# Another order for the preparation of an attention layer kernel

## The reference, cut to what matters

```python
q = (h @ Wq_c @ Wq_up).reshape(b, t, H, D).transpose(0, 2, 1, 3)      # b=2, t=1024, H=16, D=128
q = rmsnorm(apply_partial_rope(q, cos, sin), q_norm_w)
k_sw = rmsnorm(apply_partial_rope(h @ Wk, cos, sin), k_norm_w)
v_sw = h @ Wv
ck = rmsnorm(h.reshape(b, nb, M * HID) @ W_comp, k_norm_w)            # one key per block of 16 tokens
c_out = attend(q @ ck.T * scale, blocks that ended before the token, sink, ck)
sw_out = attend(50 * tanh(q @ k_sw.T * scale / 50), window of 64 tokens, sink, v_sw)
ao = (c_out + sw_out)                                                 # 4 groups of 4 heads
attn = einsum('btgf,gfi->btgi', ao, Wg).reshape(b, t, 1024) @ Wo
x = layernorm(x + attn)
x = layernorm(x + ternary_ffn(x))                                     # weight rounded to -1, 0, 1 times mean |weight|
```

## Time and profile before

| | us |
|---|---|
| median of 3 runs | 413.11 |
| lowest and highest | 410.56, 413.87 |
| the profiled execution's own time | 410.42 |
| its span, first to last instruction | 408.6 |
| PE busy | 362.8 (89%) |
| DVE busy | 329.2 (81%) |
| ACT busy | 294.3 (72%) |
| POOL busy | 283.6 (69%) |

### The profile page before, as it was taken

The page is one execution under the profiler, slowest core; times in us unless marked ns, Lnnn a source line. Parts: engine busy times, 40 slices in busy tenths (PEclk is TensorE's granted clock), DMA queues, the critical chain, the costliest instruction groups (busy, mean ns, idle before and its releaser), DMA issues. The chain is left out here.

```text
span 408.6 us, 8817 instructions
## 1 busy us (share of the span) xinstructions
PE 362.8 (89%) x3111; PEld 293.2 (72%) x3111; DVE 329.2 (81%) x683; ACT 294.3 (72%) x833; POOL 283.6 (69%) x188
## 2 busy tenths in 40 slices
PE   5995799958989899999999999979899999989882
PEld 4994676646858686877778787858686868677870
DVE  2685789677989898989989897989898989892523
ACT  3656774685877969696969695969788696958410
POOL 1844453074797979789897986887979797985802
PEclk9999799988999999999999999999999999999996
DMA  7994001887685766757675859595768777777340
GB/s 252 311 268 130 1 0 37 196 292 136 99 133 100 121 116 113 136 92 141 94 141 80 142 79 152 78 152 89 140 103 129 119 112 127 108 121 105 61 82 26
DMA packets 150284, 50.21 MB, mean 123 GB/s; under 512 B 138592, under 2 KB 148832, under 8 KB 149984
## 3 DMA queue, kind: packets, MB, share of 16 engines
q1 hardware_dynamic: 149424, 49.32, 64.4%
q10 hardware_dynamic: 816, 0.33, 0.3%
HBM read 11.87 MB, written 4.19 MB: 39 GB/s over the span
## 5 line engine op out<-in xcount | busy, mean ns | idle before, releaser
L1270 POOL TENSOR_TENSOR room_wg<-room_comp,keep 128x1024 f32<-128x1024 f32 x32 | 75.3, 2353 | 31.9 <-ACT room_comp L846 31.9
L1260 POOL TENSOR_TENSOR ao<-room_wg,ao 128x1024 f16<-128x1024 f32 x31 | 66.2, 2134 | 13.7 <-ACT ao L720 13.6
L680 PE MATMUL PS<-V,room_wg 128*128 128x129 f32 x512 | 66.2, 284 | 7.2 <-POOL room_wg L1270 4.4
L858 ACT ACTIVATE room_h<-PS,room_K 128x8 f32<-128x8 f32 (+7 forms) x256 | 70.8, 391 | 0.2 <-DVE room_K L1082 0.2
L680 PEld LDWEIGHTS PS<-V,room_wg 128*128 128x128 f32 x512 | 61.8, 198 | 11.3 <-POOL room_wg L1270 8.3
L858 ACT ACTIVATION_READ_ACCUMULATOR room_h<-PS,room_K 128x1 f32 x256 | 65.6, 278 | 0.0
L642 PE MATMUL PS<-Weff,aoT 128*128 128x256 f16 x512 | 60.8, 272 | 2.0 <-DMA aoT<-ao 2.0
L1276 POOL TENSOR_TENSOR ny<-nx,nu 128x16 f32<-128x16 f32 x16 | 46.6, 2916 | 19.8 <-DVE nx L1062 19.0
L642 PEld LDWEIGHTS PS<-Weff,aoT 128*128 128x128 f16 x512 | 49.7, 98 | 10.0 <-DMA aoT<-ao 3.1
L599 PE MATMUL PS<-room_h,kT 128*128 128x512 f16 x192 | 47.1, 380 | 10.4 <-DMA room_h<-room_K 9.9
L1060 DVE TENSOR_REDUCE ssq<-room_wg 128x8 f32<-128x1024 f32 x30 | 36.5, 1220 | 15.5 <-ACT room_wg L789 15.2
(11 more groups left out here) (185 smaller groups left out, 729.9 us busy)
## 6 DMA issues: line engine op xcount, KB each, us to landing
H<-in_L_attn_h SPq DMA_DIRECT2D x4, 512.0 KB, 6.3
room_wg<-in_L_attn_Wg SPq DMA_DIRECT2D x1, 2048.0 KB, 14.4
cw_rows<-staged SPq DMA_DIRECT2D x1, 2048.0 KB, 6.4
CW<-cw_rows SPq DMA_DIRECT2D x1, 2048.0 KB, 7.9
aoT<-ao SPq DMA_TRANSPOSE x128, 2.7
out<-room_wo SPq DMA_DIRECT2D x16, 128.0 KB, 2.1
CW<-in_L_attn_Wq_up SPq DMA_DIRECT2D x2, 512.0 KB, 13.7
room_wo<-in_L_attn_Wo SPq DMA_DIRECT2D x1, 1024.0 KB, 15.2
```

The costliest lines, as they stand in the source:

```text
L680: last = nc.tensor.matmul(pv, Pm[:, c, 2 * pr:2 * pr + 2, :], V[:, 2 * i + c, :], start=True, stop=True)
L858: last = nc.scalar.activation(Ec[:, 0:n, hd], bank(4 + hd // 8)[:, (hd % 8) * n:(hd % 8 + 1) * n], ACT.Exp, bias=mn[:, hd:hd + 1], accum_o ...
L1260: G.tensor_tensor(ao16[:, 1, c, :, :], ao[:, c, :, :], ao16[:, 0, c, :, :], ALU.subtract).then_inc(g_al, 1)
L1270: G.tensor_tensor(Pm[:, c, :, :], E[:, c, :, :], keep[:, :, :], ALU.mult).then_inc(g_mask, 1)
```

## The change

The same values are computed with the same number of matmuls. What moves:

- SP loads the up projection before the rope table and Wg instead of after them. It also waits for `s_keep` and `s_fw` before it reads `CW` back.
- ACT takes the squares of keys in two halves and the squares of values between H and KV copies; one sum of squares of Wg and both of Wo go between the WG copies. It squares the compressed key straight from PSUM, takes `square(0, ...)` ahead of the KT copies and `square(1, ...)` at the end of WE.
- DVE does the key norm's last multiplication before `latent_low(0)`. The sums and the rope of tile 0 stand ahead of the unit instead of behind it, the sums of tile 1 in step -1, and the scaling of values and of the sink factor at the end of step -1.
- POOL makes the table `below` and the splits of the sinks, and takes the first root before the window mask and the ternary weight (`local_tables`).
- PE makes `queries(1)` between WE and CW instead of at the start of step 0.

```diff
             sp.dma_start(wcomp_s[:, :, :], wcomp.rearrange("(m p) d -> p m d", p=P)).then_inc(s_comp, 16)
+            for r in range(2):
+                sp.dma_start(wqup_s[r * QC:(r + 1) * QC, :], wqup).then_inc(s_wq, 16)
             sp.dma_start(rope_s[:, :, :], rope_t).then_inc(s_tab, 16)
             sp.dma_start(wg_s[:, :, :], wg.rearrange("g (f p) i -> p (g f) i", p=P)).then_inc(s_wg, 16)
-            for r in range(2):
-                sp.dma_start(wqup_s[r * QC:(r + 1) * QC, :], wqup).then_inc(s_wq, 16)
...
                     sp.wait_ge(s_cww, 16)
+                    sp.wait_ge(s_keep, 1)
+                    sp.wait_ge(s_fw, 1)
...
                     t = i + 1
-                    if t:
+                    if t > 1:
                         queries(t)
...
                 if i == -1:
                     output_weights()
+                    queries(1)
...
+            def key_squares(n):
+
+                for g in range(4 * n, 4 * n + 4):
+                    copied(act, G_KV[g])
+                wait(act, s_tot, n)
+                nc.scalar.activation(sqk[:, TPB * n:TPB * (n + 1), :], K[:, TPB * n:TPB * (n + 1), :], ACT.Square).then_inc(s_sq, 1)
...
+                if (name, g) == ("H", 7):
+                    key_squares(0)
+                if (name, g) == ("KV", 4):
+                    value_squares(0)
+
+            key_squares(1)
+            act.wait_ge(s_wq, 32)
+            nc.scalar.activation(wqup_p[:, 0, :], wqup_s[:, :], ACT.Copy).then_inc(s_up, 1)
+            value_squares(1)
...
+            nc.scalar.activation(ck_sq, gbank(G_CK)[:, 0:D], ACT.Square, accum_out=ssk[:, NT:]).then_inc(s_cka, 1)
+            act.wait_ge(s_wg, 16)
+            for g in range(3):
+                squares(2 + g, wg_s[:, 4 * g:4 * g + 4, :])
+                latent(g)
+            latent(3)
+            square(0, 0)
+            square(0, 1)
+            for g in range(4):
+                act.wait_ge(s_ps, G_KT + g + 1)
+                nc.scalar.mul(*key_parts(g)[:2], wqk[:, 0:1]).then_inc(s_hi, 1)
+            act.wait_ge(s_setd, 1)
+            nc.scalar.mul(*key_parts(4)[:2], wqk[:, 0:1]).then_inc(s_hi, 1)
+            act.wait_ge(s_ss, 2)
+            for g in range(8):
+                if g == 1:
+                    squares(5, wg_s[:, 12:16, :])
+                if g in (3, 5):
+                    act.wait_ge(s_wo, 16)
+                    squares(6 + g // 4, wo_s[:, 4 * (g // 4):4 * (g // 4) + 4, :])
+                evac(G_WG + g, wgT[:, :, 2 * g * P:2 * g * P + 256], two(G_WG + g))
...
                 if i == -1:
                     output_weights()
+                    square(1, 0)
+                    square(1, 1)
...
-            latent_low(0)
-            copied(dve, G_CK)
-            link(V_.tensor_tensor(ck_sq, K[:, NT, :], K[:, NT, :], ALU.mult))
-            link(V_.tensor_reduce(ssk[:, NT:], ck_sq, AX.X, ALU.add))
-            V_.tensor_scalar(ckw[:, :], ssk[:, NT:], 1.0 / D, 1e-6, ALU.mult, ALU.add).then_inc(s_cks, 1)
             V_.tensor_tensor(K[:, 0:NT, :], K[:, 0:NT, :], ny[:, 0:NT].unsqueeze(2).to_broadcast([P, NT, D]),
                              ALU.mult).then_inc(s_kn, 1)
+            dve.wait_ge(s_cka, 1)
+            V_.tensor_scalar(ckw[:, :], ssk[:, NT:], 1.0 / D, 1e-6, ALU.mult, ALU.add).then_inc(s_cks, 1)
+            latent_low(0)
             dve.wait_ge(s_ckn, 1)
+            copied(dve, G_CK)
...
+            query_sums(0)
+            for hf in range(2):
+                rope_products(0, hf)
+            rope_sums(0)
...
+                        weights_rest(4, 5, 6, 7)
+                        query_sums(1)
...
                     value_weights(dve, lambda dst, src: V_.tensor_scalar(dst, src, v_unit, None, ALU.mult), 1)
+                    factors()
...
+            pool.wait_ge(s_ps, G_XC + 4)
+            G.tensor_copy(below, tables[:, P:].unsqueeze(1).to_broadcast([P, HEADS, NBLK])).then_inc(s_below, 1)
...
                 if i == -1:
-                    pool.wait_ge(s_setd, 2)
+                    pool.wait_ge(s_setn, 1)
                 if front:
                     pool.wait_ge(d_nq, t + 1)
                     G.tensor_tensor(ny[:, 0:HEADS], nx[:, 0:HEADS], nu[:, 0:HEADS], ALU.pow).then_inc(g_rs, 1)
+                if i == -1:
+                    local_tables()
```

More of the change, by code:

```diff
@@ L735, in _ @@
                     keys_values(act, nc.scalar.copy, s_kva, g)
[L737 to L745, removed]
+                if (name, g) == ("H", 5):
+                    act.wait_ge(s_sm, 2)
+                    nc.scalar.activation(e0[:, :], skm[:, :], ACT.Exp, scale=-1.0).then_inc(s_e, 1)
+                    nc.scalar.activation(e1w[:, :], skp[:, :], ACT.Exp).then_inc(s_e, 1)
+                    act.wait_ge(s_blk, 16)
+                    nc.scalar.activation(level[:, :], tables[:, 0:P], ACT.Copy).then_inc(s_sets, 1)
+                if (name, g) == ("H", 7):
[6 more added lines that the diff above has]
+            value_squares(1)
             def latent(g):
@@ L819, in results @@
                                          scale=ny[:, HEADS + 1:HEADS + 2]).then_inc(a_out, 1)
-                if front and i < 1:
-                    square(i + 1, 0)
-                if front:
+                if front and i > 0:
                     square(i + 1, 1)
@@ L1056, in step @@
                 t = i + 1
-                if front:
-                    for hf in range(2):
-                        dve.wait_ge(a_sq, 2 * t + hf + 1)
-                        V_.tensor_reduce(ssq[:, 8 * hf:8 * hf + 8], (sq if t else sq_first)[:, 8 * hf:8 * hf + 8, :], AX.X, ALU.add).then_inc(d_red, 1)
-                    dve.wait_ge(d_red, 2 * t + 2)
-                    V_.tensor_scalar(nx[:, 0:HEADS], ssq[:, :], SPREAD / D, SPREAD * 1e-6, ALU.mult, ALU.add).then_inc(d_nq, 1)
+                if front and i > 0:
+                    query_sums(t)
                 if ffn:
@@ L1086, in step @@
                     row_max(0)
-                if front:
-                    rope_products(0)
-                if first:
-                    weights_rest(0)
-                if mid:
+                    if front:
+                        rope_products(t, 0)
                     row_max(1)
-                if front:
-                    rope_products(1)
+                    if front:
+                        rope_products(t, 1)
                 if ffn:
@@ L1161, in step @@
                     query_rest(0)
-                    if first:
-                        weights_rest(5)
                     query_rest(1)
                     if first:
-                        weights_rest(6, 7)
+                        weights_rest(4, 5, 6, 7)
+                        query_sums(1)
                 def norms_of(sets):
@@ L1224, in _ @@
             G.memset(half[:, :], -0.5).then_inc(s_setp, 1)
+            pool.wait_ge(s_small, 48)
+            left = sinkb
+            for n in range(2):
+                G.tensor_copy(skh[:, n, :], left[:, :]).then_inc(s_sink, 1)
+                pool.wait_ge(s_sink, 2 * n + 1)
+                G.tensor_tensor(skr[:, n, :], left[:, :], skh[:, n, :], ALU.subtract).then_inc(s_sink, 1)
+                pool.wait_ge(s_sink, 2 * n + 2)
+                left = skr[:, n, :]
             for g in range(6, 8):
```

191 lines of the change are left out of this document (94 added, 97 removed).

## The result

| | before | after |
|---|---|---|
| median, on one chip in turn | 412.19 us (15 runs) | 415.47 us (15 runs) |
| ratio, 95% interval | | 1.0070 (1.0043 to 1.0098) |
| the same in two further comparisons | 411.60, 411.73 | 414.53, 414.19 |
| ratios there | | 1.0068 (1.0037 to 1.0098), 1.0064 (1.0028 to 1.0100) |
| the profiled execution's own time; span | 410.42; 408.6 | 414.93; 413.1 |

Three comparisons agree on some 3 us (2.5 to 3.3 by the medians, 2.8 by the mean of the ratios). A ratio leaves out the executions that are over 1.5% slower than the fastest of their kernel, so it can differ a little from the quotient of the medians. The prediction had 410.9 us, with 414.4 as the upper end of its range.

What follows compares the result with a forecast made beforehand. PE's idle waits before the second attention step were taken as the bound. First scores 0.6 us earlier plus step 0 1.6 us shorter gave -2.2 us, set on the 413.11 median: 410.9 us, range 407.4 to 414.4.

Steps and rivals of the forecast that it cites:

- first queries: Start of tile 0's query matmuls on PE: 39.9 instead of 40.61, 0.7 us earlier, behind the key norm and `latent_low(0)`.
- from there to WE: First queries to WE, carried by ACT's copies and squares: 15.9 us instead of 14.6, 1.2 us longer, WE at 55.8.
- WE to first scores: WE to the first scores: 22.6 us instead of 23.8, 1.2 us shorter; first scores at 78.4 against 79.07.
- step 0: First attention step: 1.6 us shorter (bounds 1.1 and 1.95), as mask, values and `divide` start sooner without tile 1's sums and power.
- the block: Before the first queries: POOL's 4.53 us subtraction of the up projection's low part holds up DVE's reciprocal root of the keys.
- The rope rival: Before the first queries: rope table lands at 29.1, not 25.6, shifting the key chain 3.5 us; +1.3, 414.4 us; chance 0.10.
- Both stalls: PE waits of 0.95 us in WE and 0.96 us in CW, both expected to go: 1.91 us.
- the last copy: Behind CW: the copy of its last group, formerly hidden by the queries, is uncovered and costs some 0.7 us.
- Steps 1 to 15: Attention steps behind step 0: they keep their lists and merely shift, with no growth.
- the change gives nothing: Rival: ACT's three sums of squares and a low clock in both places eat DVE's and POOL's gain; 413.1 us, chance 0.12.

## Why the prediction was wrong

Mean of three traces each (before: 79.07, 82.57, 82.72 for the first scores, and so on):

| | before | predicted | after |
|---|---|---|---|
| first queries | 41.07 | 39.9 | 41.17 |
| from there to WE | 15.5 | 15.9 | 15.9 |
| WE to first scores | 24.9 | 22.6 | 23.7 |
| step 0 | 19.53 | 17.9 | 19.68 |
| first scores of step 1 to the end | 310.5 | as before | 312.5 |

**First queries.** The mechanism was right: the block came, on the root, with 4.5 us, and moved into the path (0.17 us without the overlap; 2.4 us of the chain and 4.7 us of the total came back when the work went elsewhere). The chain from the rope products to the queries was 14.55 us in every trace of the changed kernel, against 14.3. What was mis-sized is its start, the rope table's landing: 25.6 in the prediction, 26.2 to 26.7 in the three traces (issued at 15.52 in the first, 10.7 us to landing), and the products started at 26.35 to 26.84. In sum +1.3 us. The rope rival had the right mechanism, but its bound (29.1) was too far; the latest start in any trace was 27.51. I had set the rule of the Trainium skill on `tensor_scalar` ("SBUF — State Buffer", section "Who interferes with whom") aside, as 0.4 us that no row showed. It was just such a step that took the whole 4.53 us; since any of them would have waited for the same end, the sum didn't change.

**To WE.** 15.9 predicted, 15.7 to 16.1 measured. Moving the three squares took 3.2 us off this way, just their 3.15. What the sum didn't ask for is what else they do: they open pauses of 0.5 to 0.9 us on PE right ahead of its longest dense stretch.

**WE to first scores.** Both stalls went and the last copy came (0.93 for my 0.7). (Two of the three traces of before have a third stall, 1.5 us in the middle of WE, which no trace of the changed kernel has; hence 24.9 and not 23.8 in the table.) But all three traces of the changed kernel had half clock inside WE, worth 1.6 to 1.7 us, which the sum did not hold. The clean length is 22.1 (the kernel with the old loads), better than my 22.6. I had costed the clock at the two places where the trace of before showed it low, and nowhere else. That the pauses set it off is not shown: of the eleven traces with all three squares between the copies seven had it and four had not, and it came in the kernel before, ahead of WE (53 to 57 us), in two of three traces. With two or three of the squares out of the way it did not come in three traces, which can be chance.

**Step 0.** The failed step. Prediction: the mask starts 1.5 us sooner, so values, `divide` and the next step follow, -1.6 us. After, the first mask did start 1.4 us sooner and the second values 1.1 us sooner, counted from the first scores. But the next step waits for something else: for the four transposes of the second tile's queries. The first is issued 11.0 us after the first scores before and after alike (90.11 and 91.38), and the last lands 19.5 and 19.7 us after them. I had read "the next step begins when the transposed queries have landed" off the trace, and then followed the other branch.

On the branch that counts the move did give something, and took it away again. The last two transposes also wait for the low parts of the queries, which DVE had ready 1.3 us sooner after the first scores with the sums gone (from 13.6 us on before, from 12.2 after). But with `queries(1)` in front of CW, CW ends right ahead of the first scores, and so the read-back of the value table is issued 6.7 us after them instead of 5.5 and lands 14.6 us after them instead of 13.4. For before and after, the read-back and the low parts:

```profile
84.56 0.38 SPq L394 DMA_DIRECT2D CW<-cw_rows  x1
92.63 2.36 DVE L1156 TENSOR_TENSOR room_K<-PS,room_K 128x1024 f16<-128x1024 f32 x2
```

```profile
87.06 0.38 SPq L397 DMA_DIRECT2D CW<-cw_rows  x1
92.59 2.36 DVE L1192 TENSOR_TENSOR room_K<-PS,room_K 128x1024 f16<-128x1024 f32 x2
```

And the four transposes (shortest, median and longest time of one issue in ns; first and last start) before, after, and with the read-back behind them:

```profile
L370 SPq DMA_TRANSPOSE room_h<-room_K x4: 1232/1280/1340, 90.1 to 95.2; - x4
L371 SPq DMA_TRANSPOSE room_h<-room_K x4: 1232/1325/2554, 91.4 to 96.6; - x4
L371 SPq DMA_TRANSPOSE room_h<-room_K x4: 1237/1328/1334, 90.7 to 94.7; - x4
```

The slow one is the second. It starts 12.3 us after the first scores in all three, and its 2.55 us end just behind the landing of the read-back. (That it was not slow before, where the read-back ran beside it for another 1.1 us, I can't explain.) The last is issued 16.1, 16.3 and 15.1 us after the first scores. All eighteen traces fit: with the sums in step 0 (seven) the read-back is issued at 5.5 to 5.6 us and no transpose is slow; with the sums out (ten) it is issued at 6.6 to 6.7 and one transpose takes 2.4 to 2.7 us; step 0 is 19.5 to 20.0 and 19.5 to 19.8 us. Only with the read-back out of the way was it 18.53. So of the 1.6 us 1.0 was there to be had (19.49 to 18.53), and the read-back, which the sum had at nothing, took it. Moving ScalarE's copy brought the first transpose forward by 0.8 us and took off nothing, for the same reason.

**Steps 1 to 15.** Expected to shift. They grew by 1.9 us on average of three traces, 1.3 of it in the two steps that have a stretch at half clock: step 10 in the third trace after, and the last step, which has one in all six traces. Over all timed runs the mean granted clock was 0.967 after (39 runs) and 0.970 before (111 runs), worth some 1.2 us if PE were always the bound. It isn't the whole loss: of the executions with a mean clock of 0.966 or 0.967 the median is 414.9 us after (7) and 412.3 us before (32), of those with 0.970 or 0.971 it is 413.9 (8) and 411.4 (33). Whether the change makes half clock more frequent, and by what, I can't settle.

So of the 5 us between the predicted -2.2 and the measured +2.8: 1.3 us at the first queries, 1.1 us in WE, 1.8 us in step 0, which shows in the first scores of step 1 at 100.5 instead of 96.3. The rest lies behind it. All this is counted from the first trace of before, with its second scores at 98.56. The three traces have them at 101.0 on average, later than the changed kernel's 100.5, though the timed runs have the changed kernel 2.8 us behind. Three traces, with 410.42 to 416.03 us of their own, are too few to place a difference of 3 us between two kernels. What is shown is what stood in the changed kernel's way (4.7 us the block and what hung on it, 3.5 us the squares, 1.1 us of step 0 the read-back); how its loss against the kernel before divides into stages stays open. The case "the change gives nothing" was nearest, with 0.12 of the chance; a case in which it costs had only the rope table as its mechanism.

## What to carry to other kernels

Follow every branch that ends at the point you count to: a wait that goes gives only what the next branch, here a DMA that shares its engines with another, leaves free. When work moves ahead of other work, ask which transfer now starts later, and beside what. Put GpSimd's long reads of SBUF where VectorE has nothing small to do, and side work of ScalarE in its long pauses rather than between copies that TensorE waits for. Take more than one trace of each kernel before subtracting stages: the same program had its first scores at 79.1 and at 82.7 us.

## What the runs showed of the hardware

- The block works both ways. With the subtraction on VectorE (29.21 to 31.58), one of GpSimd's products beside it took 2.79 us instead of 0.73:

```profile
28.70 0.73 POOL L1276 TENSOR_TENSOR room_wgT<-room_K,rope_s 128x256 f32<-128x256 f32 x1
29.39 2.79 POOL L1277 TENSOR_TENSOR room_wgT<-room_K,rope_s 128x256 f32<-128x256 f32 x1
```

- A pause of PE can cost twice, by its own length and by the half clock behind it. Ahead of the first queries, pauses of 0, 2.65 and 3.19 us left the eight matmuls at 2.08 to 2.09 us; one of 2.79 us gave 2.79; those of 3.43 to 5.55 us (fourteen traces) gave 3.5 to 3.8. The length alone doesn't decide: 2.79 us cost more than 3.19, and ahead of the last step's scores the clock fell behind a pause of 2.08 us (changed kernel, first trace) and stayed up behind one of 2.27 us (third trace).
- A transpose can be slow beside a 2 MB transfer. With the read-back issued behind them, each of the four took 1.2 to 1.3 us to issue and 3.2 to 3.4 us from issue to landing. With it issued 4.3 us ahead of them (changed kernel, three traces), the second took 2.4 to 2.6 us to issue, and the slowest landed 4.6 to 4.9 us after its issue. With it 5.5 us ahead (kernel before) none was slow.
